# Mixing products on two 64-row halves of the array instead of one 128-row block-diagonal product

## The chip, the cores and the metric

The kernel runs on one core of a Trainium2 chip. The metric is the device time of one execution in microseconds, as the median of several runs; lower is better. Before the change it is 798.31 us (three runs, 797.32 to 798.47).

## The reference, cut to what matters

The input x is (128, 32, 512). Two residual blocks are added to it: an attention block over mixed channels, and a state-space convolution with a quantised linear layer. The change touches only the first step of the attention block, the mixing of the 32 channels of each batch element by a 32x32 matrix that is chosen by the element's condition:

```python
def cond(x, condition, weights):
    W = weights[condition]                       # (128, 32, 32)
    return jnp.einsum('bct,bcd->bdt', x, W)      # (128, 32, 512)

x = x + attn(cond(x, itok_B_0_15, weights), ...)  # compressed queries and keys, 32 heads, softmax over 32 tokens
x = x + ffn(ssm_convolution(x, itok_B_8_3872, ...), ...)
```

For each batch element this is a product over 32 channels; its result h, with the 512 features as contraction, feeds the projections to the compressed queries (192) and the compressed keys and values (128).

## The kernel before, in words

It is written engine by engine, with the order of work on each engine fixed by hand and semaphores between them (`pe`, `act`, `dve`, `pool`, `sp` are TensorE, ScalarE, VectorE, GpSimd and the DMA-issuing SyncE). The batch is cut into 8 sets of 16 elements, and each set has two groups of 16 heads, so the main loop has 16 units u. In a unit TensorE folds queries with the head weights (`fold`, L755), takes the value products of the unit before (`values`, `value_block`, L829), the scores (`scores`, L804) and the output products of the unit before (`output`, L629 to L631 through the helper `three`, which forms a product in three parts of high and low halves).

Mixing is done 8 elements at a time: call i of `mixed_x` (L645), i from 0 to 15, two calls for each set. The input tile `x_in` holds (element, channel) on the 128 partitions, 4 elements with 32 channels each, for two groups g of 4 elements. The matrices come as the tile `mix`, built as a block-diagonal 128x128 matrix (4 blocks of 32x32) for each g. For each of the four feature tiles tt and each g, 128 columns of `x_in` are the stationary operand and the 128x128 block-diagonal `mix` is streamed past it: 8 f32 matmuls per call, 4 into each of two PSUM banks. A bank holds two feature tiles, and when its four products are done `h_ready` is raised; this is in the middle of the call for the first bank, at its end for the second. ScalarE copies each bank to `h_high` (`mixed_high`, L1144), VectorE subtracts to get `h_low` (`mixed_low`, L1463). `project_ca` then contracts h with the compression weights in four steps tt (L629 to L631), waiting for the low parts as it goes; `project_ab` and `project_kv` follow.

Where this stands on TensorE: calls 0 and 1 at the start, behind `first_mixing` (L943) and transposes of the weights (L956), and ahead of three tiny bias products (L963 to L965) and `project_ca(0)`. Calls 2 to 15 stand as seven pairs in the odd units, in the order `output(u-1, 0)`, `mixed_x(i)`, `mixed_x(i+1)`, `output(u-1, 1)`, `output(u-1, 2)`, `project_ca`, `project_ab`, `project_kv`, `output(u-1, 3)`. The output products and the projections use the whole array, 128 rows by 128 columns. The folds and value products work on 64-row halves, with the two halves e alternating and each writing a bank of its own; so do `values_half` (L858, f32, in the last unit) and `turned_weights` (L718, f32, 64x64 parts). Other lines that the text speaks of: L699 `products` (head weights, at the start), L740 a transpose of parameters, L949 matmuls on ones ahead of all work, L1232 the copy of the value products, L1614 the low part of the transposed compression weights, for which call 1 waits.

Of the kernel before, what the change touches and what calls it, by code (L numbers as in the profile page):

```python
# [13 lines left out]
P = 128  # L14
# [6 lines left out]
TT = T // P  # L21
# [8 lines left out]
HT = ST // 2  # L30
# [36 lines left out]
def f(ap):  # L67

    return ap.bitcast(F32)
# [57 lines left out]
def build(nc, d, out):  # L127
    mem = Memory(nc)
    scratch_taps = [nc.dram_tensor(f"taps_scratch{n}", (C, KROW), F32, kind="Internal").ap() for n in range(3)]
    ps = mem.ctx.enter_context(nc.psum_tensor("ps", [P, 8, 512], F32))  # L130

    m = Map(nc)
    t = m.tile
# [34 lines left out]
    x_in = [t(f"x_in{n}", [P, 2, T], at=at) for n, at in enumerate((x_at, h_at + 4 * KB))]  # L168
    h_high = t("h_high", [P, 2, TT, HT], F32R, at=qt_at + 16 * KB)
    h_low = t("h_low", [P, 2, TT, HT], F32R, at=qt_at + 24 * KB)  # L170
# [42 lines left out]
    def small(name, shape, dt=F32):  # L213
# [46 lines left out]
                for n in range(R)]  # L260
# [30 lines left out]
    s = {n: mem.sem(n) for n in weight_names + attention_names + taps_names + ffn_names + channel_names}  # L291
# [12 lines left out]
    MIX_BANK = (BT, BS)  # L304
# [12 lines left out]
    pT_two = lambda h, m_: pT_last[h][:, 2 * m_:2 * m_ + 2].rearrange("p n b a c -> p n (b a c)")  # L317
    half_of = lambda tile, h, m_, e: (tile[:, 2 * m_:2 * m_ + 2, 4 * h:4 * h + 4, :]
                                      .rearrange("p n a (b e c) -> p e n (a b) c", b=2, e=2)[:, e])
    two_of = lambda tile, u, m_: tile[:, 2 * m_:2 * m_ + 2, u - LAST].rearrange("p n b a c -> p n (b a c)")  # L320
    EARLY = B - SB
    by_h = lambda n, hs: parT[:, n, hs].unsqueeze(2).unsqueeze(3).broadcast_to([P, HC, 4, LA])
# [3 lines left out]
    def x_arrived(i):  # L326
        return s[("x_loaded", "x1_loaded")[i % 2]], 16 * (i // 2 + 1)

    def mix_of(i):
        return mix if i % 2 == 0 else mix_first if i == 1 else mix_odd  # L330
# [11 lines left out]
    with nc.Block() as block:  # L342
# [284 lines left out]
        def _(pe):  # L627
            def three(out, lh, ll, rh, rl, start=True, stop=True):
                pe.matmul(out, lh, rh, start=start, stop=False)  # L629
                pe.matmul(out, lh, rl, start=False, stop=False)  # L630
                return pe.matmul(out, ll, rh, start=False, stop=stop)  # L631

            def mixed_x(i):
                pe.wait_ge(*x_arrived(i))
                pe.wait_ge(s["mix_ready"], i + 1)
                if i >= 2:
                    pe.wait_ge(s["s_taken"], 4 * (i - 1) + 2 if i % 2 == 0 else 4 * (i - 1))
                elif i == 1:
                    pe.wait_ge(s["wcT_done"], 2)
                for n in range(2):  # L640
                    for t_ in range(2):
                        for g in range(2):
                            tt = 2 * n + t_
                            o = t_ * HT + g * P
                            mm = pe.matmul(ps[:, MIX_BANK[i % 2] + n, o:o + P], x_in[i % 2][:, g, tt * P:(tt + 1) * P],  # L645
                                           mix_of(i)[:, g, :], start=True, stop=True)
                    mm.then_inc(s["h_ready"], 1)

            def project_ca(k):
                if k == 0:  # L650
                    pe.wait_ge(s["wcT_done"], 2)
                for tt in range(TT):
                    if tt % 2 == 0:
                        pe.wait_ge(s["h_low_done"], 4 * k + 3 + tt // 2)
                    mm = three(ps[:, BZ + 1, :], wcT_high[:, tt, 1, :], wcT_low[:, tt, 1, :], h_high[:, :, tt, :],
                               h_low[:, :, tt, :], tt == 0, tt == TT - 1)
                mm.then_inc(s["qca_ready"], 1)
# [296 lines left out]
            for m_ in range(3):  # L954
                for t_ in range(TT):
                    mm = pe.transpose(ps[:, BS + m_, t_ * P:(t_ + 1) * P], wc_raw[:, m_, t_ * P:(t_ + 1) * P], ident[:])  # L956
                mm.then_inc(s["wcT_ready"], 1)
            first_mixing(1)
            mixed_x(0)
            mixed_x(1)  # L960
            pe.wait_ge(s["bias_in"], 16 * 6)
            pe.wait_ge(s["const_ready"], 2)
# [3 lines left out]
                      stop=True).then_inc(s["bias_ready"], 1)  # L966
# [19 lines left out]
            for u in range(1, LAST):  # L986
# [15 lines left out]
                i = u + 1  # L1002
# [127 lines left out]
        def _(act):  # L1130
# [8 lines left out]
            act.dma_start(bkv_c[:], col(d["L0_attn_bkv_c"])).then_inc(s["bias_in"], 16)  # L1139

            def mixed_high(i):
                for n in range(2):
                    act.wait_ge(s["h_ready"], 2 * i + n + 1)
                    act.copy(h_high[:, i % 2, 2 * n:2 * n + 2, :].rearrange("p a n -> p (a n)"),  # L1144
                             ps[:, MIX_BANK[i % 2] + n, :]).then_inc(s["h_high_done"], 1)

            def projected_ca(k):
                if k == 0:
# [169 lines left out]
            for u in range(1, LAST):  # L1318
# [29 lines left out]
                elif u >= 3:  # L1348
                    k = (u - 3) // 2
# [21 lines left out]
                i = u + 1  # L1371
# [76 lines left out]
        def _(dve):  # L1448
            rows = lambda n: flat(sc[:, n]).rearrange("p (r c) -> p r c", c=C)
# [8 lines left out]
                dve.wait_ge(s["step"], steps[0])  # L1458

            def mixed_low(i):  # L1460
                for n in range(2):
                    dve.wait_ge(s["h_high_done"], 2 * i + n + 1)
                    dve.tensor_tensor(h_low[:, i % 2, 2 * n:2 * n + 2, :].rearrange("p a n -> p (a n)"),  # L1463
                                      ps[:, MIX_BANK[i % 2] + n, :],
                                      f(h_high[:, i % 2, 2 * n:2 * n + 2, :].rearrange("p a n -> p (a n)")),
                                      ALU.subtract).then_inc(s["h_low_done"], 1)

            def projected_ca(k):
# [230 lines left out]
            for u in range(1, LAST):  # L1699
# [29 lines left out]
                i = u + 1  # L1729
# [113 lines left out]
            for c in range(C + LAG):  # L1843
# [30 lines left out]
                if 0 <= c - 3 < C - 1:  # L1874
                    k = c - 3
# [16 lines left out]
            k = C - 1  # L1892
# [40 lines left out]
```

## Time and profile before

| | |
|---|---|
| median of three runs | 798.31 us |
| the profiled execution | 791.97 us |
| its span, first to last instruction | 790.2 us |
| TensorE matmuls busy | 766.3 us (97%), 6857 records |
| TensorE weight loads busy | 640.5 us (81%) |
| VectorE, ScalarE, GpSimd busy | 626.0, 417.9, 273.0 us |
| mean granted TensorE clock | 0.994 of full |

The times below are of the one profiled execution, on its own clock from the start of the span. A record's duration is its latency: matmuls and weight loads are pipelined, so that 16 records of 275 ns can follow each other every 112 ns. An f32 matmul leaves two records of matmul and two of weight load, one with high and low parts (fp32r) one of each. In a row of the timeline, "x16" are 16 records that were merged, and the second number runs from the start of the first to the end of the last. "64*128" is the part of the array in use, rows by columns. "Idle before <- issue" is time in which the engine waited for nothing that the profile shows.

### The profile page before, as it was taken

The page shows a single profiled execution, that of the slowest core. Times are in us where ns is not written, and L with a number is a line of the kernel's source. Part 1 is how long each engine was busy: PE and PEld are TensorE (multiplying, and loading weights), DVE is VectorE, ACT ScalarE, POOL GpSimd, SP SyncE. Part 2 cuts the span into 40 slices and gives each one's busy share as a digit, 9 for nine tenths or more (in the row PEclk, how much of TensorE's full clock was granted, in tenths as well). Part 3 has the DMA queues.
Part 4 walks back from the last instruction along what each step waited for, and adds up shares of the span by engine and source line. Part 5 has one row for each costly group of instructions (what it writes and reads, how often), then busy time and mean ns, then how long its engine had stood idle before and what let it go on. Part 6 is the DMA issues. An engine that isn't in the chain of part 4 may idle for free.

```text
span 790.2 us, 16966 instructions
## 1 busy us (share of the span) xinstructions
PE 766.3 (97%) x6857; PEld 640.5 (81%) x6857; DVE 626.0 (79%) x1104; ACT 417.9 (53%) x749; POOL 273.0 (35%) x258
## 2 busy tenths in 40 slices
PE   9999999999999999999999999999999799999996
PEld 7777688778788878877887888788787689999996
DVE  5677989998998695768677666957788778888887
ACT  2575547656583776566555837565684332222221
POOL 4001403131131204271311313020133488888871
PEclk9999999999999999999999999999999999999999
DMA  9911000210111020001301000202035448888861
GB/s 226 235 52 28 4 28 2 54 32 1 25 31 31 1 55 16 16 1 36 62 1 28 26 32 1 55 1 58 2 107 127 134 116 203 202 202 203 202 136 68
DMA packets 61293, 56.10 MB, mean 71 GB/s; under 512 B 25584, under 2 KB 48160, under 8 KB 61216
## 3 DMA queue, kind: packets, MB, share of 16 engines
q1 hardware_dynamic: 58944, 54.33, 28.1%
q8 instruction: 55, 0.90, 0.5%
q0 software_dynamic: 1056, 0.49, 0.3%
q10 hardware_dynamic: 1216, 0.19, 0.2%
q14 instruction: 22, 0.18, 0.1%
HBM read 41.91 MB, written 8.63 MB: 64 GB/s over the span
## 4 chain that ended last, share of the span: by engine, by line
PE 81%; DVE 11%; ACT 3%; POOL 2%; issue 2%; DVEq 0%
PE ps L755 28%; PE ps L629 9%; PE ps L630 8%; PE ps L631 8%; PE ps L804 7%; DVE z_low L1520 4%; PE ps L1103 4%; PE ps L645 4%; PE ps L1104 4%; PE ps L1072 2%; PE ps L829 1%; PE ps L718 1%; ACT qt L1208 1%; DVE sc L1509 1%; PE ps L1060 1%
## 5 line engine op out<-in xcount | busy, mean ns | idle before, releaser
L553 POOL TENSOR_TENSOR pT_low<-pT,pT_high 128x512 fp32r<-128x512 f32 x60 | 81.3, 1356 | 360.4 <-ACT pT_high L1222 360.4
L1208 ACT ACTIVATE qt<-ps,m_bias 128x512 f32<-128x512 f32 x242 | 155.4, 686 | 74.9 <-PE ps L755 74.9
L755 PE MATMUL ps<-q_high,m_high 64*128 64x512 f32 x768 | 154.6, 396 | 0.5 <-issue 0.5
L755 PE MATMUL ps<-q_high,m_low 64*128 64x512 f32 x768 | 151.2, 387 | 0.0
L755 PE MATMUL ps<-q_low,m_high 64*128 64x512 f32 x768 | 108.6, 387 | 0.0
L755 PEld LDWEIGHTS ps<-q_high,m_high 64*128 64x128 f32 x768 | 73.0, 184 | 22.7 <-issue 5.9
L755 PEld LDWEIGHTS ps<-q_low,m_high 64*128 64x128 f32 x768 | 73.1, 184 | 14.3
L755 PEld LDWEIGHTS ps<-q_high,m_low 64*128 64x128 f32 x768 | 73.2, 184 | 13.1
L1520 DVE TENSOR_TENSOR z_low<-ps,z_high 128x512 fp32r<-128x512 f32 x120 | 73.2, 680 | 10.8 <-ACT z_high L1232 10.7
L1213 ACT ACTIVATE sc<-sc 128x512 f32<-128x512 f32 x60 | 37.6, 631 | 63.4 <-DVE sc L1501 63.4
L1438 ACT COPY x1T_far<-ps 128x128 f32<-128x128 f32 x32 | 8.5, 267 | 103.7 <-PE ps L1072 103.7
L1232 ACT CAST z_high<-ps 128x512 fp32r<-128x512 f32 x120 | 60.6, 620 | 1.9 <-PE ps L829 1.5
L804 PE MATMUL ps<-qt,kv 128*32 128x256 f32 x960 | 56.0, 386 | 3.0 <-DVE z_low L1520 2.9
L629 PE MATMUL ps<-z_high,wvT_high 128*128 128x512 f32 (+1 forms) x136 | 55.0, 405 | 0.0
L615 POOL TENSOR_TENSOR x_s<-x,fb 128x512 f32<-128x512 f32 x32 | 43.6, 1362 | 31.7 <-DVE x L1851 31.7
L1509 DVE TENSOR_TENSOR sc<-sc,row_stat 128x512 f32<-128x512 f32 x60 | 50.6, 844 | 2.1
L630 PE MATMUL ps<-z_low,wvT_high 128*128 128x512 f32 (+1 forms) x136 | 52.2, 384 | 0.0
L631 PE MATMUL ps<-z_high,wvT_low 128*128 128x512 f32 (+1 forms) x136 | 52.1, 383 | 0.0
L829 PE MATMUL ps<-pT_high,c_tok 64*128 64x256 f32 x480 | 46.9, 288 | 5.1 <-issue 3.1
L804 PEld LDWEIGHTS ps<-qt,kv 128*32 128x32 f32 x960 | 34.8, 111 | 20.1 <-issue 6.8
L1526 DVE TENSOR_SCALAR qt<-ps,m_bias 128x512 f32<-128x512 f32 x14 | 10.5, 748 | 47.1 <-PE ps L755 46.9
L829 PEld LDWEIGHTS ps<-pT_high,c_tok 64*128 64x128 f32 x480 | 39.4, 188 | 9.3 <-issue 7.3
(299 smaller groups left out, 1821.1 us busy)
## 6 DMA issues: line engine op xcount, KB each, us to landing
x_in<-in_x SPq DMA_DIRECT2D x16, 512.0 KB, 4.1
x_s<-in_x SPq DMA_DIRECT2D x32, 256.0 KB, 5.5
out<-res SPq DMA_DIRECT2D x31, 256.0 KB, 3.3
toep_high<-taps_scratch SPq DMA_DIRECT2D x32, 192.0 KB, 4.4
toep_low<-taps_scratch SPq DMA_DIRECT2D x32, 192.0 KB, 4.8
c_tok<-ctok SPq DMA_DIRECT2D x64, 64.0 KB, 2.1
toep_far<-taps_scratch SPq DMA_DIRECT2D x32, 64.0 KB, 5.6
wq_nope<-in_L_attn_Wq_up SPq DMA_DIRECT2D x2, 768.0 KB, 10.0
```

The costliest lines, as they stand in the source:

```text
L553: pool.tensor_tensor(flat(pT_low[:, n]), flat(pT[:, n]), f(flat(pT_high[:, n])), ALU.subtract).then_inc(s["pl_done"], 1)
L615: pool.tensor_tensor(tiles(x_s[c % RX]), backwards(x1[c % 2]), tiles(fb), ALU.add).then_inc(s["x1b_done"], 1)
L629: pe.matmul(out, lh, rh, start=start, stop=False)
L630: pe.matmul(out, lh, rl, start=False, stop=False)
L631: return pe.matmul(out, ll, rh, start=False, stop=stop)
L755: mm = pe.matmul(ps[:, fold_bank(u, j) + e, :], weights[rows, (GH * g + j) // 2, c, :], moving[c][rows, :], start=start, stop=stop)
L804: mm = pe.matmul(ps[row:row + 32, SBANK[n], (b // 2) * 256:(b // 2 + 1) * 256], kv[:, tok], qt[:, half:GH:2, tok], start=True, stop=True)
L829: mm = pe.matmul(ps[:, banks[e], cols], c_tok[rows, x, 2 * n + b, :], p_[rows], start=(r == 0), stop=(r == 2))
L1208: act.activation(qt[:, j, :], ps[:, fold_bank(u, j) + j % 2, :], ACT.Identity, bias=m_bias[:, h:h + 1]).then_inc(s["qt_done"], 1)
L1232: act.copy(z_high[:, n].rearrange("p a (b e c) -> p e b a c", b=2, e=2)[:, e], ps[:, banks[e], :].rearrange("p (b a c) -> p b a c", b=2, a=GP)
L1509: dve.tensor_tensor(rows(n), rows(n), wide(n), ALU.mult).then_inc(s["norm_done"], 1)
L1520: dve.tensor_tensor(part(z_low), ps[:, banks[e], :].rearrange("p (b a c) -> p b a c", b=2, a=GP), f(part(z_high)), ALU.subtract).then_inc( ...
```

## The change

`mixed_x` takes, for each feature tile and group, two products in place of one: one on rows 0 to 63 and one on rows 64 to 127, each with its own 64x64 part of the diagonal of `mix` (two blocks of 32x32). Half e writes to bank e, 64 columns for each (tt, g). A call has 16 matmuls in place of 8, and a bank now holds all four feature tiles for half of the elements, so that both banks are complete only at the end of the call. `mixed_high` and `mixed_low` go by halves e and write their results in runs of 64 elements to the same places in `h_high` and `h_low` as before. `project_ca` waits once, for all low parts of both calls, in place of waiting at tt = 0 for three of the four and at tt = 2 for the last.

```diff
+    h_of = lambda tile, i, e: (tile[:, i % 2].rearrange("p t (g e c) -> p e t g c", g=2, e=2)[:, e])
+    h_bank = lambda i, e: ps[:, MIX_BANK[i % 2] + e, :].rearrange("p (t g c) -> p t g c", t=TT, g=2)
@@ mixed_x(i)
-                for n in range(2):
-                    for t_ in range(2):
-                        for g in range(2):
-                            tt = 2 * n + t_
-                            o = t_ * HT + g * P
-                            mm = pe.matmul(ps[:, MIX_BANK[i % 2] + n, o:o + P], x_in[i % 2][:, g, tt * P:(tt + 1) * P],
-                                           mix_of(i)[:, g, :], start=True, stop=True)
-                    mm.then_inc(s["h_ready"], 1)
+                for tt in range(TT):
+                    for g in range(2):
+                        for e in range(2):
+                            rows, o = slice(64 * e, 64 * e + 64), tt * P + 64 * g
+                            mm = pe.matmul(ps[:, MIX_BANK[i % 2] + e, o:o + 64], x_in[i % 2][rows, g, tt * P:(tt + 1) * P],
+                                           mix_of(i)[rows, g, rows], start=True, stop=True)
+                            if tt == TT - 1 and g == 1:
+                                mm.then_inc(s["h_ready"], 1)
@@ project_ca(k)
+                pe.wait_ge(s["h_low_done"], 4 * k + 4)
                 for tt in range(TT):
-                    if tt % 2 == 0:
-                        pe.wait_ge(s["h_low_done"], 4 * k + 3 + tt // 2)
@@ mixed_high(i)
-                for n in range(2):
-                    act.wait_ge(s["h_ready"], 2 * i + n + 1)
-                    act.copy(h_high[:, i % 2, 2 * n:2 * n + 2, :].rearrange("p a n -> p (a n)"),
-                             ps[:, MIX_BANK[i % 2] + n, :]).then_inc(s["h_high_done"], 1)
+                for e in range(2):
+                    act.wait_ge(s["h_ready"], 2 * i + e + 1)
+                    act.copy(h_of(h_high, i, e), h_bank(i, e)).then_inc(s["h_high_done"], 1)
@@ mixed_low(i)
-                for n in range(2):
-                    dve.wait_ge(s["h_high_done"], 2 * i + n + 1)
-                    dve.tensor_tensor(h_low[:, i % 2, 2 * n:2 * n + 2, :].rearrange("p a n -> p (a n)"),
-                                      ps[:, MIX_BANK[i % 2] + n, :],
-                                      f(h_high[:, i % 2, 2 * n:2 * n + 2, :].rearrange("p a n -> p (a n)")),
+                for e in range(2):
+                    dve.wait_ge(s["h_high_done"], 2 * i + e + 1)
+                    dve.tensor_tensor(h_of(h_low, i, e), h_bank(i, e), f(h_of(h_high, i, e)),
                                       ALU.subtract).then_inc(s["h_low_done"], 1)
```

## Rows read from the trace of the kernel before

**Rows 1.** The page, busy time, share of the span and records.
```profile
PE 766.3 (97%) x6857; PEld 640.5 (81%) x6857; DVE 626.0 (79%) x1104; ACT 417.9 (53%) x749; POOL 273.0 (35%) x258
```
**Rows 2.** Chain of waits in order of time: start, us, what (seven pieces like the second).
```profile
12.28 3.83 PE ps L645 x32
...
98.59 3.57 PE ps L645 x32
```
**Rows 3.** Waits of TensorE: total us, times, longest.
```profile
PE ps L829 <- issue: 3.1, 3, 1.4
...
PE ps L858 <- DVE z_low L1800: 2.6, 1, 2.6
```
**Rows 4.** Timeline of the first pair in the loop: start us, us, engine, line.
```profile
98.20 0.39 PE L631 MATMUL ps<-z_high,wvT_low 128*128 128x512 f32 x1
98.43 1.95 PE L645 MATMUL ps<-mix,x_in 128*128 128x128 f32 x16
100.10 1.87 PEld L645 LDWEIGHTS ps<-mix_odd,x_in 128*128 128x128 f32 x16
102.23 0.40 PE L630 MATMUL ps<-z_low,wvT_high 128*128 128x512 f32 x1
```
**Rows 5.** Timeline of weight loads, `first_mixing` (32 columns streamed).
```profile
10.31 1.87 PEld L943 LDWEIGHTS ps<-cond_w,chooser 128*128 128x128 f32 x16
```
**Rows 6.** Timeline of weight loads, a bias product (32 rows, one column streamed).
```profile
16.44 0.29 PEld L965 LDWEIGHTS ps<-ones,bkv_raw 32*128 32x128 f32 x2
```
**Rows 7.** Groups by shape: busy us, mean ns of one record.
```profile
L645 PEld LDWEIGHTS ps<-mix_odd,x_in 128*128 128x128 f32 x112 | 13.1, 192 | 0.0
...
L858 PEld LDWEIGHTS ps<-pT_last,c_full 64*128 64x128 f32 x64 | 3.8, 187 | 3.9 <-issue 3.1 <-DVE pT_last L1795 0.7
...
L718 PEld LDWEIGHTS ps<-ident,wq_rope 64*64 64x64 f32 x192 | 6.9, 135 | 0.0
```
**Rows 8.** Timeline around `values_half`, between full-array products.
```profile
606.07 0.40 PE L631 MATMUL ps<-z_high,wvT_low 128*128 128x512 f32 x1
606.40 1.86 PEld L858 LDWEIGHTS ps<-pT_last,c_full 64*128 64x128 f32 x32 [0.36 <-issue]
608.72 0.40 PE L630 MATMUL ps<-z_low,wvT_high 128*128 128x512 f32 x1
```
**Rows 9.** Timeline of weight loads, `turned_weights` (64 columns streamed).
```profile
26.50 0.43 PEld L718 LDWEIGHTS ps<-ident,wq_rope 64*64 64x64 f32 x12
```
**Rows 10.** Timeline where a fold follows an output product.
```profile
114.02 0.39 PE L631 MATMUL ps<-z_high,wvT_low 128*128 128x512 f32 x1
...
114.68 0.40 PE L755 MATMUL ps<-q_high,m_low 64*128 64x512 f32 x2
```
**Rows 11.** Groups by shape: a copy with scattered writes.
```profile
L1232 ACT CAST z_high<-ps 128x512 fp32r<-128x512 f32 x120 | 60.6, 620 | 1.9 <-PE ps L829 1.5
```
**Rows 12.** Timeline behind the first pair in the loop.
```profile
102.19 0.59 ACT L1144 CAST h_high<-ps 128x512 fp32r<-128x512 f32 x1 [0.31 <-PE ps L645]
102.81 0.69 DVE L1463 TENSOR_TENSOR h_low<-ps,h_high 128x512 fp32r<-128x512 f32 x1 [0.20 <-ACT h_high L1144]
104.51 0.19 PEld L629 LDWEIGHTS ps<-h_high,wcT_high 128*128 128x128 f32 x1
```
**Rows 13.** Timeline of the start, from the weights' low part to the projection.
```profile
12.66 1.28 DVE L1614 TENSOR_TENSOR wcT_low<-ps,wcT_high 128x512 fp32r<-128x512 f32 x2
15.87 0.69 DVE L1463 TENSOR_TENSOR h_low<-ps,h_high 128x512 fp32r<-128x512 f32 x1 [0.38 <-ACT h_high L1144]
16.75 0.50 PE L629 MATMUL ps<-h_high,wcT_high 128*128 128x512 f32 x1
16.77 0.69 DVE L1463 TENSOR_TENSOR h_low<-ps,h_high 128x512 fp32r<-128x512 f32 x1 [0.20 <-ACT h_high L1144]
```
**Rows 14.** Timeline of the start: the wait that follows, on TensorE.
```profile
29.29 0.88 PE L699 MATMUL ps<-wq_nope,wk 128*64 128x193 f32 x8 [0.70 <-DVE m_bias L1564]
```
**Rows 15.** Stretches: us, busy (records) of PE, PEld, DVE, ACT, POOL, clock, DMA, GB/s.
```profile
617.00:620.00 3.00, 3.00 (x16) 3.00 (x16) 2.96 (x6) 1.22 (x3) 1.71 (x2) 0.50 0.25 89
```

## The prediction

> **What bounds the kernel now.** I read the page's totals first: TensorE's matmuls fill 97% of the span, so little of anything else can be the limit [rows 1]. The chain of waits says the same by line: the mixing products (L645) hold 4% of it, and its pieces in order of time show them whole, 3.83 us for the first two calls and 3.57 us for each of the seven later pairs, 28.8 us in all [rows 2]. The waits of TensorE are small: the longest total is 3.1 us [rows 3]. So what the mixing section takes on TensorE is added to the time one for one, and what is only slower on ScalarE or VectorE costs nothing until TensorE waits for it.
>
> What sets the pace inside the section? Each f32 matmul of L645 leaves two records of matmul and two of weight load, so a call (8 matmuls) has 16 of each. In the timeline 16 loads take 1.87 us with a last one of 0.19: 1.68 / 15 = 112 ns from one to the next [rows 4]. The matmul streams 128 columns. L943, also 128x128 in f32 but with only 32 columns streamed, has the same row, 16 loads in 1.87 us at full clock [rows 5]. A quarter of the columns at the same pace: there the weight load is the limit, about 110 ns per record, and the number of streamed columns is not. L645 sits on that same bound.
>
> Does a load of fewer rows take less? L965 loads 32 rows by 128 columns and streams one column; its two loads take 0.29 us, so the second starts 0.10 after the first [rows 6]. The single loads agree: 192 ns with 128 rows (L645), 187 with 64 rows and 128 columns (L858), 135 with 64x64 (L718) [rows 7]. Rows don't matter, columns do. The Trainium skill states it too, in "TensorE: Matmul & The Clock Gate", section "LDWEIGHTS (loading the stationary operand)": the load goes by the columns and a 32x128 load takes as long as a 128x128 one. No run here has a 64x128 f32 load with 64 streamed columns, so the page bears on the case; the trace agrees where it can.
>
> **The change part by part.**
> 1. Products. Removed per pair of calls: 16 matmuls of 128 rows by 128 streamed columns (32 records). Added: 32 matmuls of 64 rows by 64 streamed columns (64 records). The stationary tile still has 128 columns, so each load stays at about 107 ns, and there are twice as many. What can save them is that the two row halves work side by side. L858 shows that: 64x128 tiles, halves alternating, 32 loads in 1.86 us: (1.86 - 0.19) / 31 = 54 ns per record [rows 8]. L858 streams 128 columns, ours 64; by the finding above the load is the bound in both, so I take 54. Bounds: below, L718, which streams 64 columns in alternating halves: 12 loads in 0.43 with a last of 0.135, 27 ns per record, but with 64-column loads, half as long [rows 9]; above, 112, if the halves took turns. With 54: 64 x 0.054 = 3.46 us against 32 x 0.112 = 3.58.
> 2. Switching between full and half array. Before, the section's neighbours are full-array matmuls as L645 is. From the last matmul ahead of it (98.20) to the second one behind (102.23) is 4.03 us; less two at the ordinary 0.23, the section costs 3.57 [rows 4]. L858 lies between the same neighbours: from 606.07 to 608.72 is 2.65, less 0.46 is 2.19, of which 32 x 0.054 = 1.73 is its own pace. 0.46 us is left for going into the half array and out [rows 8]. The entry shows again where a fold follows an output product: from 114.02 to 114.68, 0.66 for what takes 0.46 [rows 10]. Bounds: nothing, if other work covered it (no row shows that), and 0.7, twice the idle mark of 0.36 ahead of L858's first load. New section: 3.46 + 0.46 = 3.92, so +0.35 us per pair and, for the seven pairs in the loop, +2.4 us.
> 3. Drains. Same four copies and four subtractions per pair, on the same 512 elements per partition; the outputs now lie in runs of 64 elements. Scattered writes of this sort are in the trace: z_high 620 ns against 590 for h_high [rows 11, 12]. 30 ns x 32 on ScalarE, 1.0 us, none of it on the path. What moves is when they start: a bank used to be ready in the middle of a call, now both are ready at its end, some 0.1 us apart.
> 4. The wait of project_ca. It needed three of four low parts to begin and the fourth six matmuls later; now it needs all four. In the loop 12 output matmuls (2.7 us) lie between. The last low part ended at 102.81 + 0.69 = 103.50, the projection's first load is at 104.51 [rows 12]. With the change: the last load of the second call starts at 98.53 + 63 x 0.054 = 101.93, its bank is ready some 0.41 later as now (101.78 against 102.19), two copies (0.59) and the second subtraction end at 104.2; the projection comes up at 104.86. Slack 0.6 us: hidden, seven times. VectorE's maxima behind the subtractions start 0.7 us later, 0.35 against TensorE; they feed a softmax that TensorE reads only behind the next fold. I take 0, bound 1 us over the loop.
> 5. The same wait at the start. Here only three bias products (0.7 us) lie between. Before, the projection began at 16.75, after the third low part (15.87 + 0.69 = 16.56), and the fourth ended at 17.46, ahead of its use six matmuls of 0.23 later [rows 13]. Now: the second call can't begin before 14.05, since it waits for wcT_low (12.66 + 1.28, and 0.1 until it starts); its last load is at 15.73, the banks are ready at 16.05 and 16.15, the copies end at 16.64 and 17.26, the subtractions at 17.36 and 18.07. The projection begins at 18.1, not 16.75: +1.3 us. Queued behind the waiting instruction are all of TensorE's later products. After the projections the chain runs over q_high, q_low and VectorE's exponential to the 0.70 us wait at 29.29, and q_low itself follows the projection, so this wait doesn't absorb the delay; behind 29.29 it is TensorE nearly alone [rows 14]. Bounds: +0.4, if later work makes room or the copies start before the call's end as I have it; +2, if VectorE or the copies queue up behind each other.
>
> DMAs: the loads of x_in wait on the same counts of h_ready, a few tenths later and far ahead of their use. GpSimd's mixing tiles likewise. Nothing.
>
> **Sum.** 2.4 + 1.3 = +3.7 us. The profiled execution took 791.97 us (span 790.2), so 795.7 for a profiled one; the runs' median lies 6.3 us above it at 798.31, and I carry the difference over: 802.0 us.
>
> **Rivals.**
> A, the split is faster: a load of half the rows takes half the time, or hides behind the other half's. Then the pace is L718's 27 to 29 ns per record: 64 x 0.029 + 0.46 = 2.32 against 3.57, -1.25 x 7 = -8.8; the start loses some 0.5 (the second call is bound by the same wait and ends 0.8 earlier). -8.3 us: 790.0. It decides the sign from below 46 ns per record: there 7 x (64 x 0.046 + 0.46 - 3.57) = -1.2 makes up for the start. For it: L718's pace; no row has our form. Against it: L965, and that L943 gains nothing from fewer streamed columns. The Trainium skill, "TensorEngine Tiling (Array Packing)", section "Theoretical Speedup", gives up to 2x where the contraction is 64 or less; by that factor alone the section would be 1.8 us. L858 reaches such a factor only against f32 work of as many streamed columns and half the rows, while here the number of loads doubles; I give the rule this rival's chance.
> B, the halves don't work side by side (one after the other at 107 to 112 ns): 64 x 0.107 + 0.46 = 7.3, +3.7 x 7 and +3.5 at the start, +29 us: 827. L858 speaks against it [rows 8].
> C, no difference: switching is cheaper next to L645's short matmuls (0.2 per pair, so 7 x 0.1) and the start's delay is partly regained (0.4). +1.1 us: 799.4. It decides wherever the rest of TensorE's queue makes room; against it stand rows 8 and 10, which show the gap each time.
> D, the idle time at the start brings the half clock. The trace has it once, for about 3 us, close behind the wait of 2.6 us of L858 [rows 3, 15]. Some 1.5 us on top, 803.5, and the wait here would be half as long.
>
> **Chances.** Forecast (+1.6 to +5 us) 0.66, D 0.06, B 0.03, C 0.14, A 0.11. A measurement tells about 0.2% (1.6 us) from no change. Slower is the forecast with D and B, 0.75; same is C, 0.14; faster is A, 0.11. The range 798.3 to 806.0 leaves out A, B and a small part of C; the forecast's own error (pace 52 to 58 ns, switch 0.3 to 0.6, start 0.4 to 2) is +1 to +7.
>
> **What would show it.** Step 1: L645 with 512 records, 64*128 with 64 columns, a single load still near 187 ns and 32 loads of a call in about 1.9 us; loads of 100 ns or a call in 1.1 us is A, 3.5 us is B. Step 2: an idle mark of about 0.35 ahead of the first load of each pair and of the output product behind it. Steps 4 and 5: no wait on h_low in the loop, and one of about 1.3 us ahead of the first projection. I am wrong in the whole if the chain's share of L645 falls.

## The result, and the profile after

| | median | lowest to highest |
|---|---|---|
| before | 798.16 us (5 executions) | 797.24 to 798.47 |
| after | 806.51 us (5) | 803.32 to 807.16 |

The change makes the kernel slower: after to before is 1.0101, interval [1.0080, 1.0122], so +8.35 us (+6.4 to +9.7). Forecast were +3.7 us and 802.0, with a range up to 806.0: the sign is right, the size more than double, and the median lies half a microsecond outside the range. The profiled execution took 806.54 us with a span of 804.7.

One thing has to be known to read the numbers below. The kernel before takes about 791 us on two of the chips used in the experiments and about 801 on two others. The trace of before shown above, 791.97 us, is of an execution of the first kind; the executions in the table, at 798, are more like the second, and which chip they ran on is not on record. Each experiment is therefore compared with the kernel before on its own chip.

The page of the changed kernel, busy time of each engine and the chain of waits by line, answers to [rows 1]:
```profile
PE 775.6 (96%) x7113; PEld 645.1 (80%) x7113; DVE 625.3 (78%) x1104; ACT 415.9 (52%) x749; POOL 272.8 (34%) x258
PE ps L756 28%; PE ps L631 9%; PE ps L632 8%; PE ps L633 8%; PE ps L805 7%; DVE z_low L1518 4%; PE ps L646 4%; PE ps L1104 4%; PE ps L1105 4%; PE ps L1073 2%; PE ps L719 1%; PE ps L830 1%; ACT qt L1208 1%; DVE sc L1507 1%; PE ps L1061 1%
```
There are 256 more records of matmul (7113 against 6857), as the change says: mixing is now L646, with 512 records instead of 256. The chain in order of time (start, us, what) answers to [rows 2]:
```profile
102.94 4.88 PE ps L646 x55
179.44 3.13 PE ps L646 x51
251.22 3.67 PE ps L646 x61
...
542.73 3.72 PE ps L646 x64
```
Only the last pair is whole (x64); in the other six the chain begins 3 to 13 records late, since something interrupts the call there. The last pair, in the timeline, answers to [rows 4]:
```profile
542.33 0.40 PE L633 MATMUL ps<-z_high,wvT_low 128*128 128x512 f32 x1
542.65 1.86 PEld L646 LDWEIGHTS ps<-mix,x_in 64*128 64x128 f32 x32 [0.37 <-issue]
544.43 1.87 PEld L646 LDWEIGHTS ps<-mix_odd,x_in 64*128 64x128 f32 x32
546.71 0.39 PE L632 MATMUL ps<-z_low,wvT_high 128*128 128x512 f32 x1
```
From 542.33 to 546.71 is 4.38; less two ordinary products at 0.23 the section costs 3.92, to the hundredth what the forecast had, with its idle mark of 0.37 ahead of the first load. The second mark that the forecast named, ahead of the output product behind the pair, is not in the trace. The first pair is another thing:
```profile
101.59 0.83 PE L646 MATMUL ps<-mix,x_in 64*128 64x64 f32 x9
102.94 1.56 PE L646 MATMUL ps<-mix,x_in 64*128 64x64 f32 x23 [0.52 <-issue]
104.38 3.43 PE L646 MATMUL ps<-mix_odd,x_in 64*128 64x64 f32 x32
```
TensorE stops after nine records and goes on half a microsecond after the last has ended, and then the second call takes 3.43 us for what takes 1.95 elsewhere. The first is a stall, the second half clock. Both stand at the start too (engines PE, ScalarE, PE; compare [rows 13]):
```profile
13.80 1.74 PE L646 MATMUL ps<-mix_first,x_in 64*128 64x64 f32 x26
16.41 0.55 PE L646 MATMUL ps<-mix_first,x_in 64*128 64x64 f32 x6 [0.86 <-issue]
16.46 2.05 ACT L1145 CAST h_high<-ps 128x512 fp32r<-128x512 f32 x4 [5.44 <-remote]
19.71 0.76 PE L631 MATMUL ps<-h_high,wcT_high 128*128 128x512 f32 x1 [2.04 <-DVE h_low L1463]
```
ScalarE begins its four copies at 16.46, though the first two banks were complete when call 0 ended at about 13.9 (11.93 + 2.00); so all copies and subtractions lie behind one another, and the first projection starts at 19.71 instead of 16.75. The stretches behind it (columns as in [rows 15]; 1.00 in the clock's column is 2.4 GHz, 0.50 is 1.2):
```profile
19.00:23.00 4.00, 3.29 (x8) 2.67 (x9) 1.64 (x5) 0.00 (x0) 0.00 (x0) 0.57 1.12 273
105.00:112.00 7.00, 7.00 (x38) 6.03 (x37) 5.32 (x10) 2.16 (x4) 0.00 (x0) 0.53 0.24 75
```
The waits (us in all, times, longest):
```profile
DVE sc L1493 <- remote: 13.3, 7, 2.4
ACT h_high L1145 <- remote: 5.4, 1, 5.4
PE ps L646 <- issue: 3.2, 7, 0.9
PE ps L631 <- DVE h_low L1463: 2.0, 1, 2.0
```
"remote" means that no instruction in the trace accounts for the release. The trace of before, of an execution of 791.97 us, has no such row.

### The profile page after: what moved, and what is told of

The parts are those of the page before. It is cut to its first block, busy times and chain, and to the rows that moved or that the text cites. A ratio compares the mean times of both kernels' runs of the same rounds, so it can differ in the third digit from the quotient of the medians.

```text
span 804.7 us, 17478 instructions
## 1 busy us (share of the span) xinstructions
PE 775.6 (96%) x7113; PEld 645.1 (80%) x7113; DVE 625.3 (78%) x1104; ACT 415.9 (52%) x749; POOL 272.8 (34%) x258
## 4 chain that ended last, share of the span: by engine, by line
PE 80%; DVE 12%; ACT 3%; issue 2%; POOL 2%; another core or an unknown queue 1%; DVEq 0%
PE ps L756 28%; PE ps L631 9%; PE ps L632 8%; PE ps L633 8%; PE ps L805 7%; DVE z_low L1518 4%; PE ps L646 4%; PE ps L1104 4%; PE ps L1105 4%; PE ps L1073 2%; PE ps L719 1%; PE ps L830 1%; ACT qt L1208 1%; DVE sc L1507 1%; PE ps L1061 1%
## 5 line engine op out<-in xcount | busy, mean ns | idle before, releaser
L1493 DVE STREAM_TRANSPOSE sc<-ps 128x512 f32<-128x512 f32 x60 | 39.0, 691 | 13.7 <-remote 13.3
```

## Experiments

The theories. The forecast F: 0.35 us of switching per pair and 1.3 us at the start. D, as in the prediction: the start's wait brings half clock behind it. G: the stalls come with GpSimd's four gathers of mixing weights (`gather`, an indirect DMA each), whose time coincides with the mixing calls, and the split calls suffer more from them. I: they come with the supply of TensorE's instructions, of which the split doubles the number in mixing. Of the gathers in the trace after, the last ahead of the first pair starts at 101.06 and ends at 102.00, 0.94 us before the stall ends; ahead of the last pair, which has no stall, none runs.

**1. The same two kernels on another chip.**

> The kernel before, once more, for its trace. Its profiled execution was 791.97 us and its other runs 797.2 to 798.5, so something of some 6 us differs from execution to execution. If TensorE and the engines that wait for it stall while GpSimd's gathers run (theory G, seen in the trace after the change), a run near 798 should show such a stall or a stretch at half clock, some 1 to 3 us each, that the first trace lacks; a run near 792 shows none. If the stalls belong to the change alone, this trace is the first one again in every stretch, whatever its total.

> The changed kernel once more, beside the kernel before on one chip. With the gathers moved it took 795.8 us there, +4.35 over before. If the gathers are what stalled it (theory G): +8 again, near 799.5 to 800, with the same gaps of 0.6 to 1 us in the mixing calls of six units. If the stalls belonged to the chip or the execution and not to the gathers: within 1 us of 795.8 and no such gap.

Measured, beside 791.4 us for the kernel before: before again 790.89 us (one execution); after again 797.07, ratio 1.0080 [1.0059, 1.0102], +5.7 us. Its six executions fall into two sets: 795.40, 795.56, 795.93 with a mean clock of 0.994 or more, and 798.20, 800.03, 800.09 with 0.990 and 0.988. The profiled one is of the first set. Its start:
```profile
14.26 2.00 PE L646 MATMUL ps<-mix_first,x_in 64*128 64x64 f32 x32
16.88 1.29 DVE L1463 TENSOR_TENSOR h_low<-ps,h_high 128x512 fp32r<-128x512 f32 x2 [0.56 <-ACT h_high L1145]
18.32 0.47 PE L631 MATMUL ps<-h_high,wcT_high 128*128 128x512 f32 x1 [1.35 <-DVE h_low L1463]
```
and its first and last pair in the chain:
```profile
98.71 3.72 PE ps L646 x64
...
530.88 3.72 PE ps L646 x64
```
No call is interrupted, no copy released late, the wait at the start is 1.35 us. This is the forecast's kernel. From the first pair to the last it takes 432.17 us (530.88 - 98.71), where the kernel before takes 429.93, from 98.59 in [rows 2] to the last piece of its chain:
```profile
528.52 3.57 PE ps L645 x32
```
That is 2.24 us over six pairs, 0.37 each. So neither the stalls nor the half clock come with every execution of the changed kernel.

**2. The gathers moved.** GpSimd waits at the start until both first mixing calls are done, and in the loop it gathers one unit later, in the odd units. The same edit is made to both kernels:
```
             pool.wait_ge(s["row_ready"], 1)
+            pool.wait_ge(s["h_ready"], 4)
             gather(2)
...
-                    if u + 4 < 2 * NS:
-                        gather(u + 4)
-                        gather(u + 5)
+                if u % 2 == 1 and u + 3 < 2 * NS:
+                    gather(u + 3)
+                    gather(u + 4)
```


> The changed kernel with GpSimd's gathers of the mixing matrices moved: at the start behind the two mixing calls, in the loop by one unit, so that none runs within some 20 us of a mixing section. Theory G (in the gathers' time TensorE's semaphore raises are held back until about 0.9 us after the last one, and TensorE stops when its queue is full): the stalls of 0.6 to 1 us in six pairs, the late release of ScalarE at the start (16.46 us) and the two half-clock stretches go; the kernel falls from 806.5 to about 802, where my sum had it, all eight mixing sections at 3.5 us of their own. Rival I (instruction supply: the short matmuls outrun what TensorE's sequencer delivers): stalls stay where they are and the time stays within 1 us of 806.5.

> The same move of the gathers in the kernel before, as control. Theory G with the stall belonging to the change: no difference from before within 0.2%. If gathers hold TensorE up in the kernel before as well, in the executions that take 798 and not 792: -3 to -6 us. Rival I: no difference.

Measured: after with moved gathers 795.78 us, 1.0070 [1.0047, 1.0094], +4.35 us; before with moved gathers 791.56, 1.0007 [0.9989, 1.0025]. The trace of the first has no stall, the wait at the start is 1.34 us and the projection starts at 18.14 (forecast: 18.1). But the unmoved kernel in experiment 1 had no stalls on this chip either, so the pair doesn't decide on G.

**3. Twice the matmuls without the halves.** All 128 rows, 64 columns streamed, so 16 matmuls per call that can't lie side by side:
```
-        x_in[i % 2][rows, g, tt * P:(tt + 1) * P], mix_of(i)[rows, g, rows], ...
+        x_in[i % 2][:, g, tt * P:(tt + 1) * P], mix_of(i)[:, g, rows], ...
```


> The changed kernel with each of its 16 matmuls per call over all 128 rows (64 columns streamed, same banks, drains and waits); the block-diagonal zeros make the result the same. No half-array mode and no pairing. By my load-bound reading each record takes 112 ns: 64 x 0.112 = 7.2 us per pair against 3.58, +25 us over the loop and some +3.5 at the start: about 827 us. If streamed columns set the pace and not the load: 64 x 0.054 = 3.5 us per pair, about 800. If the stalls come from the half-array mode, none is seen here; if they come from the gathers alone, they are seen here too.

Measured: 821.57 us, 1.0396 [1.0354, 1.0437], +30.1 us. Its two calls of one pair, weight loads:
```profile
103.73 3.77 PEld L646 LDWEIGHTS ps<-mix,x_in 128*128 128x128 f32 x32
107.42 3.65 PEld L646 LDWEIGHTS ps<-mix_odd,x_in 128*128 128x128 f32 x32
```
(3.65 - 0.19) / 31 = 112 ns from one load to the next, with 64 columns streamed instead of 128: the pace does not depend on the streamed columns, and the halves are what brings it to 55. This is what rival B would have been, priced at +29. It has no bearing on I: as many instructions and no stall, but on this chip the changed kernel has none either.

**4. The start as before.** Calls 0 and 1 in the kernel before's form, with its waits; with the gathers where they were (e6), and with them moved (e7); and, with the gathers moved, with only the second call of each pair split (e8):
```
+                if i < 2:            # e8: if i < 2 or i % 2 == 0
+                    ... the eight 128-row products, h_ready after each bank of two tiles
+                    return
...
-                pe.wait_ge(s["h_low_done"], 4 * k + 4)
+                if k > 0:
+                    pe.wait_ge(s["h_low_done"], 4 * k + 4)
                 for tt in range(TT):
+                    if k == 0 and tt % 2 == 0:
+                        pe.wait_ge(s["h_low_done"], 3 + tt // 2)
```


> The changed kernel with calls 0 and 1 (products, banks, copies) and the waits of the first projection as they were before; the seven pairs of the loop stay split. My sum: the start's +1.3 us goes and the seven pairs' +2.4 stays, if no stall comes in. Theory G: the stall of 2.5 us and the half-clock stretch at the start go as well, so 3 to 5 us under the changed kernel, the stalls of the loop stay. Rival (the start's delay is regained later): no difference from the changed kernel.

> Both: gathers moved, start as before, seven pairs split. My sum leaves the switching alone: 7 x 0.35 = +2.4 us over before (about 793.9 where before takes 791.4), each pair's section 3.92 us from the matmul ahead to the second one behind, less two of 0.23. Rival (switching costs nothing, all of it was stalls and start): +0 within 0.2%.

> As e7, but in each pair only the second call is split; the first has its 8 full-array products. One way in and one way out of the half array remain. If switching is the cost: 16 x 0.112 + 32 x 0.054 + 0.46 = 3.98 us per pair, +0.41 x 7 = +2.9 us over before, as much as with both calls split or a little more. If the cost lies in the number of short matmuls: half of e7's, +1.2 us.

Measured: 793.84 us, 1.0033 [1.0020, 1.0046], +2.5; 793.95, 1.0035 [1.0023, 1.0048], +2.6; 793.90, 1.0035 [1.0022, 1.0048], +2.5. The term for the loop was +2.4. With only one call of two split it is the same: the cost is one switch in and one out per pair and does not go with the number of short matmuls. The chain of the second kernel of the three (mixing is L657 there) shows the excess in the pairs:
```profile
98.62 3.72 PE ps L657 x64
...
530.64 3.72 PE ps L657 x64
```
432.02 against 429.93: 0.35 us per pair.

**5. A third comparison, for the clock.**

> The kernel before a third time, for its trace and clock. Where its runs are near 791 the last trace showed two half-clock stretches and no stall. If this chip or this time gives runs near 798 (as the first comparison did, 797.2 to 798.5), theory G expects stalls of TensorE about the gathers or more half-clock stretches in the trace; if it is neither, every stretch is a little longer.

> The changed kernel a third time. The first comparison had +8.35 us with stalls in six pairs, the second +5.7 us with none in its trace. If the kernel before is near 791 here: +4.3 in the executions with clock 0.994 and up to +9 in those with 0.988, no stall. If it is near 798: +8, stalls in the trace (theory G).

> The changed kernel with the gathers moved, a third time. Before near 798 and theory G right: +4 us over before and no stall, where the changed kernel has +8 and stalls. Before near 791: +4.3 as last time, no more spread than 795 to 798, so about 1.5 us under the changed kernel's median, if the half-clock executions go with the gathers.

Measured: before 790.78 us, ratio 0.9993; after 797.96, 1.0077 [1.0060, 1.0094], +6.7; after with moved gathers 795.93, 1.0067 [1.0043, 1.0091], +4.7. With the gathers moved the changed kernel's median is 1.3 us lower in experiment 2 and 2.0 here, but the intervals overlap both times, so a gain is not shown. The profiled execution of the second took 797.81 and shows what sets the two sets of experiment 1 apart, the granted clock behind the start's wait and once more ahead of the first pair:
```profile
18.00:22.00 4.00, 4.00 (x12) 3.14 (x11) 0.35 (x2) 0.00 (x0) 0.00 (x0) 0.57 1.11 235
90.00:98.00 8.00, 6.40 (x78) 3.97 (x78) 7.62 (x14) 4.56 (x9) 3.97 (x5) 0.79 0.01 2
```
The same two stretches of the changed kernel's profiled execution in experiment 1, 795.93 us:
```profile
18.00:22.00 4.00, 3.69 (x16) 3.09 (x17) 1.24 (x5) 0.58 (x1) 0.00 (x0) 1.00 1.13 264
90.00:98.00 8.00, 6.50 (x92) 4.80 (x93) 7.66 (x14) 4.52 (x9) 4.79 (x5) 1.00 0.01 4
```
The second stretch is not bound to the change. Here is the trace of before that the prediction was made from, at the same place:
```profile
90.00:98.00 8.00, 7.75 (x92) 4.73 (x90) 7.71 (x13) 3.35 (x7) 5.16 (x6) 0.79 0.03 8
```
Time from the first mixing product to the first pair in the loop, from the timelines, gives the price (clock 18 to 22 and 90 to 98 in brackets): before in this experiment 84.87 us (1.00, 1.00), before as shown above 86.31 (1.00, 0.79), after in experiment 1 86.26 (1.00, 1.00), after here 89.32 (0.57, 0.79). So the start's wait costs 86.26 - 84.87 = 1.4 us, and a stretch of half clock about 1.5: 86.31 - 84.87 = 1.4 and (89.32 - 86.26) / 2 = 1.5. In ten traces with the old start, of all experiments, the clock from 18 to 22 us is 1.00 each time. And the stretch that before has too stands behind a wait of TensorE as long as the new one at the start, 1.37 us (timeline, before as shown above):
```profile
89.63 0.50 PE L829 MATMUL ps<-pT_high,c_tok 64*128 64x256 f32 x4 [1.37 <-issue]
```

**6. On a chip where before takes 801 us.** The changed kernel, and the same with a filler: three f32 products of 128x512 on a tile that lies ready, issued before `project_ca(0)` so that TensorE is busy in the wait:
```
+            for _ in range(3):
+                pe.matmul(ps[:, BX, :], busy[:, 0:P], busy[:], start=True, stop=True)
             project_ca(0)
```


> The changed kernel a fourth time. Before near 791: executions near 795.6 with a clock of 0.994 and others near 798 and 800 with 0.990 and 0.988, as twice before; the traces of the latter have a half-clock stretch of 3.4 us behind the wait at the start. Before near 798: stalls about the gathers, and +8.

> The changed kernel with three f32 matmuls of 512 columns on the tile of ones (0.43 us a record pair half, some 2.6 us in all) in the wait ahead of the first projection; TensorE would be idle there for 1.3 us. Theory D (the wait at the start brings the half clock in about half of the executions): the filler costs some 1.3 us that the wait doesn't hide, and no execution has a half-clock stretch near 18 us: nearly all within 796.5 to 797.5, none at 800. Rival (the half clock comes for another reason): the same spread as without, 795 to 800, moved up by 1.3 us.

> The kernel before, one look in the same state as the two others, for the length of its sections in that state: as in its first trace if it is near 791; with stalls if it is near 798.

Measured, beside 801.29 us for before: after 809.97, 1.0116 [1.0092, 1.0140], +8.7 us; with the filler 810.61, 1.0125 [1.0098, 1.0151], +9.3; before, one execution, 802.29. The trace of before on this chip has what I had taken for a trait of the changed kernel:
```profile
DVE sc L1495 <- remote: 14.4, 6, 2.9
PE ps L645 <- issue: 1.2, 2, 0.7
PE ps L629 <- DVE h_low L1463: 1.0, 1, 1.0
```
```profile
98.07 0.73 PE L645 MATMUL ps<-mix,x_in 128*128 128x128 f32 x5
99.52 1.39 PE L645 MATMUL ps<-mix,x_in 128*128 128x128 f32 x11 [0.72 <-issue]
101.04 2.02 PE L645 MATMUL ps<-mix_odd,x_in 128*128 128x128 f32 x16
```
The stalls are in both kernels, so the doubled number of instructions, theory I, is not what brings them. Between the first pair and the last they cost the kernel before 9.3 us (439.20 against 429.93), the changed one 8.9 in the trace of the result (441.06 against 432.17), half clock in the first pair included. What before does not have is half clock at 18 us (1.00 in its trace). The filler did take that away in its profiled execution, 18 to 22 us:
```profile
18.00:22.00 4.00, 4.00 (x13) 2.31 (x13) 2.83 (x7) 0.71 (x2) 0.00 (x0) 1.00 1.09 247
```
and that one is its fastest at 806.22, with a mean clock of 0.996. But the median is no better, and the mean clocks of its five other executions, 0.986 to 0.993, are no higher than without the filler (0.986 to 0.992): a busy TensorE in the wait did not rid them of half clock. And in the trace of after on this chip the clock is down to half from about 18.2 us on, when the wait has just begun (18.18 to 20.11):
```profile
18.00:19.00 1.00, 0.17 (x2) 0.09 (x1) 1.00 (x3) 0.91 (x2) 0.00 (x0) 0.61 1.11 217
20.11 0.77 PE L631 MATMUL ps<-h_high,wcT_high 128*128 128x512 f32 x1 [1.93 <-DVE h_low L1463]
```
Ahead of it lie two idle times, 0.32 and 0.49 us, and the small bias products. So half clock goes with the new start, but that the wait alone brings it, as D has it, is not shown.

**7. The gathers moved, on a chip where before takes 801 us.**

> The kernel before with the gathers moved away from the mixing sections. On a chip where before takes 798 to 802, its trace has stalls of TensorE in the odd units 1 to 11, where gathers run, and none in 13, where none does. Theory G: with the gathers moved it falls to about 792 to 795 there (the stalls cost 1 us each in six units, and the start's), and no scores transpose of the odd units waits. If the stalls only go with that stretch of the program and not with the gathers: no difference. On a chip where before takes 791: no difference, as before.

> The changed kernel with the gathers moved, on the same chip as e15. Theory G: +4 to +6 over e15, since only switching, the start's wait and its half clock remain, and 6 to 9 us under the changed kernel where before takes 798 to 802. If the stalls stay: about +8.5 over before as the changed kernel has it.

> The changed kernel beside the two others: +8 to +9 where before takes 798 to 802, +4.3 to +6.7 where it takes 791.

Measured, beside 801.11 us: before with moved gathers 800.87, 0.9990 [0.9971, 1.0009]; after with moved gathers 808.63, 1.0083 [1.0053, 1.0112], +7.5; after 811.01, 1.0127 [1.0104, 1.0150], +9.9. In the trace of the first the gathers of the start run from 16.74 to 21.7, and most of the unexplained waits have gone with them, from the scores (14.4 us in experiment 6, 3.3 here) to ScalarE's ctok and z_high:
```profile
ACT ctok L1174 <- remote: 5.6, 1, 5.6
ACT z_high L1233 <- remote: 5.4, 3, 1.8
DVE sc L1496 <- remote: 3.3, 3, 1.2
```
So G holds in that the stalls go where the gathers go, and falls in that moving them gains the kernel before nothing: the stalls cost as much elsewhere. The trace of the second, after with moved gathers, has no late release at the start and a wait of 1.35 us as in experiment 1, and half clock all the same, 0.50 in 18 to 22 us; it begins before the wait (17.33 to 18.67) is over:
```profile
18.00:22.00 4.00, 3.33 (x8) 2.68 (x9) 1.60 (x5) 0.00 (x0) 3.08 (x4) 0.50 1.10 282
```
The trace of after, 808.52 us, has the start at its worst (PE, then the clock of the stretches):
```profile
16.53 0.50 PE L646 MATMUL ps<-mix_first,x_in 64*128 64x64 f32 x5 [0.99 <-issue]
19.82 0.77 PE L631 MATMUL ps<-h_high,wcT_high 128*128 128x512 f32 x1 [2.09 <-DVE h_low L1463]
```
```profile
18.00:22.00 4.00, 2.18 (x5) 1.82 (x6) 2.75 (x7) 0.62 (x2) 0.00 (x0) 0.54 1.12 262
22.00:26.00 4.00, 4.00 (x12) 3.10 (x11) 0.00 (x0) 0.62 (x1) 0.00 (x0) 0.61 1.12 204
```
From the first mixing product to the first pair it takes 92.52 us, where before on such a chip takes 86.03 (experiment 6): 6.5 us at the start alone.

**8. The start as before, on such a chip.** The kernel of experiment 4 with the gathers unmoved.

> The changed kernel with the kernel before's form in calls 0 and 1, so that the start is as before. On a chip where the kernel before takes 798 us or more: if the excess over the forecast stands at the start (call 0 released late, a wait on h_low of 2 us, 3.4 to 6.8 us at half clock), this kernel loses only the switching, +2.5 to +3.5 us, where the changed kernel lost 7.5 to 10 in four comparisons. If the split form itself is stalled more in every pair, +7 or more. On a chip where the kernel before takes 791 us: +2.5 again.

Measured: 805.62 us (12 executions), beside 801.32, 1.0053 [1.0037, 1.0068], +4.3 us (+3.0 to +5.4). The same chip gave the changed kernel +9.9 (+8.3 to +12.0) in experiment 7; the intervals don't touch. So the new start costs 5.6 us there by the medians of the two experiments, against 3.2 in experiment 1 (5.7 less 2.5) and a forecast of 1.3. Its trace has full clock at the start, and the first pair 85.57 us behind the first mixing product:
```profile
18.00:22.00 4.00, 4.00 (x19) 3.16 (x18) 2.52 (x7) 1.31 (x2) 0.00 (x0) 1.00 1.14 252
```
The 4.3 that are left are 1.8 more than the 2.5 of experiment 4, but the two intervals overlap (+3.0 to +5.4 here, +1.6 to +3.6 there), so that the 1.8 are real is not shown. The profiled execution takes 444.11 us from the first pair to the last, more than any other of its kind. It has half clock there, from the second pair on, behind a stall of 0.92 us:
```profile
174.00:182.00 8.00, 8.00 (x50) 7.04 (x49) 5.76 (x11) 2.78 (x5) 0.00 (x0) 0.57 0.21 66
```
That stalls cut deeper into split calls does not explain it. In the four traces of split pairs on such chips that have no half clock in this part of the program, it takes 439.61 to 441.72 us (experiments 6 and 7), and in the two of before 439.20 and 439.55. That is 0.1 to 2.5 more, and switching alone gives 2.1 to 2.2. Half clock behind a stall inside a split call stands in the trace of the result and in this one, and in neither of the two of before; whether the split makes it more likely, so few traces do not tell. No version beats the kernel before.

## Why the prediction was wrong in size

**What bounds the kernel, and that nothing hides the mixing section:** right. The clean excess in the pairs, 2.2 us over six, came out in the time one for one (+2.5 for seven).

**Step 1, products:** right. Single loads of 188 ns (forecast 187), 32 in 1.86 us, 55 ns per record (54), and 112 with all rows. A split that doubles the count of loads only buys back what it doubled; rival A was never near (B neither).

**Step 2, switching, +0.35 us per pair:** right, 0.35 to 0.37 in the traces, +2.5 and +2.6 in the times. That it does not go with the number of split calls (e8) was not in the prediction. The Trainium skill, "TensorEngine Tiling (Array Packing)", lists under "Key Properties" that switching modes requires a drain; the idle mark of 0.37 ahead of the first load of the last pair fits it. In these runs going in and out makes the pair a third of a microsecond longer than before.

**Steps 3 and 4, drains and the wait in the loop at 0:** right. A copy takes 591 ns on the average and a subtraction 686, so that even the 30 ns for scattered writes did not come, and the projections in the loop never wait for h_low; the waits list has it once, at the start.

**Step 5, the start, +1.3 us:** the step that failed. The mechanism is as it was told, and where nothing else happens the numbers are too: projection at 18.32 and 18.14 (18.1), a wait of 1.35 (1.3), 1.4 us of time. But the term was left too small: the start cost 3.2 us by the medians of experiments 1 and 4, and 5.6 by those of 7 and 8. Two things came on top.

First, half clock. I had it as rival D, at 1.5 us and a chance of 0.06 beside the forecast's 0.66. The price of one stretch was right; the chance was not. It begins in the wait or within 1.1 us behind it in all six profiled executions of the changed kernel (gathers moved or not, without the filler) that took over 797 us, in neither of the two below 796, and in none of the ten traces with the old start; by the mean clocks half of the six executions of experiment 1 had more of it than the others. So it goes with the new start; that the wait alone causes it is not shown, since the filler did not remove it and on the slower chips the clock fell before the wait had ended.

I had written that the trace of before has half clock once, at 617 us, behind a wait of 2.6, and that the wait here would be half as long. That reading was wrong. The trace has it from 91 us on as well, and behind 1.37 us: the longest of L829's waits, which [rows 3] list with 1.4; and once more in its last microseconds. With the execution of before in experiment 5, which has the same wait and full clock, the chance comes to about a half, an estimate from two traces, and at 1.5 us it would have added some 0.8 us.

Second, the start is sensitive to a late release, since all four low parts are needed: on the chips where TensorE's calls are interrupted and ScalarE is released only at 16.46, the projection comes at 19.7 to 20.1 and not 18.1, and half clock lasts up to twice as long (0.54 in 18 to 22 us and 0.61 in 22 to 26). Before, on such a chip, it needs three low parts and begins at 17.78, waiting 1.0. This share is small: from the first mixing product to the projection the trace of the result takes 7.78 us and before in experiment 6 takes 5.74, 2.0 more, where on the other chips it is 1.3 more (5.94 in experiment 1, 4.63 in the trace of before).

**The measurement base:** wrong. I added 6.3 us to the profiled execution's time as a constant. The slower executions of the kernel before that were traced (experiments 6 and 7) have stalls in them that the trace of before does not show, so it was another condition of the same program and no constant. A cost worked out in the one need not hold in the other: the change cost 5.7 and 6.7 us in the one, 8.7 and 9.9 in the other.

Adding up for the result, as an estimate, since experiment 8 ran on a chip of its own: a kernel with the old start loses 4.3 us there, 2.5 of it switching and 1.8 from a cause not shown and within the intervals; the other 4.05 of the 8.35 are the start, 1.3 of them forecast. The traces say much the same of the start and divide it. From the first mixing product to the first pair the result's trace takes 3.6 us more than before in experiment 6 (89.66 and 86.03): 2.0 up to the projection, of which the forecast had 1.3 and the late release makes 0.7, and 1.6 behind it, where its one stretch of half clock lies. The trace of after in experiment 7 has 2.2 and 4.3, with half clock three times as long in all.

Of the rivals, D is the one that happened on top of the forecast, though its trigger stays open. C's room in the rest of the queue was not there: the wait is 1.35 us, and 1.4 arrive at the first pair.

## What to carry over

Packing f32 products with few streamed columns into half arrays pays only if the number of weight loads does not grow: count loads times pace first, and add what a visit to the half array costs, here a third of a microsecond per pair whether one call or both were split. Where TensorE is the bound, a new wait near the start is not priced by its length alone: look in the whole trace for stretches of half clock, note how short the waits are beside which they stand, and put the price with its chance into the sum. If the profiled execution and the median differ by more than the cost you forecast, ask what is in the slower ones before you carry the difference over.

## What the runs showed of the hardware that was not expected

- The same program on one core takes 791 us on two of the chips and 801 on two others. The traces of the slower ones have stalls that end shortly after GpSimd's indirect DMAs and take 9.3 us more from the first pair to the last: TensorE stops in the middle of a call with nothing to wait for (0.5 to 1.0 us), and an engine that waits for a matmul that has ended is released 2.5 us late (ScalarE at 16.46 for call 0, whose records end at 13.9). The stalls moved with the gathers, and the kernel before was no faster for it. What holds the releases back is not settled; a version without indirect DMAs was not tried.
- A wait of 1.35 us can be followed by a stretch of half clock, and the same wait in another execution of the same kernel by none: 0.79 and 1.00 in 90 to 98 us for before, 0.57 and 1.00 in 18 to 22 us for after. Each such stretch, 3.4 us long, cost 1.4 to 1.5 us. In the trace of after in experiment 6 half clock begins with a wait and not behind it, and in that of experiment 8 it begins at 174.4 us, 1.6 us after a stall of only 0.92 has ended.
